# DLRM tower on one core: first two one-hot tables as a couple, and another order of the interaction stage

## The reference

```python
e = jnp.stack([tbl_0[ids[:, 0]], ..., tbl_25[ids[:, 25]]], axis=1)
T = jnp.concatenate([dense[:, None, :], e], axis=1)        # 512 x 27 x 128
Z = jnp.einsum('bnd,bmd->bnm', T, T)                       # all pairs
z = Z[:, iu0, iu1]                                         # 351 pairs, upper triangle
h = jnp.concatenate([z, r_dense], axis=1)
h = jnp.maximum(h @ W_top1 + b_top1, 0.0)                  # 479 -> 512
h = jnp.maximum(h @ W_top2 + b_top2, 0.0)                  # 512 -> 256
y = h @ W_top3                                             # 256 -> 1
```

## Time and profile before

| | us |
|---|---|
| median of 3 runs (118.52, 598.5, 118.72) | 118.72 |
| the profiled execution's own time | 118.53 |
| its span | 116.7 |
| PE busy in the span | 108.4 (93%) |
| DVE busy | 85.6 (73%) |
| ACT busy | 80.9 (69%) |
| POOL busy | 65.3 (56%) |
| DMA, mean over the span | 152 GB/s |
| a gather of POOL, median from issue to landing | 4.1 |
| a move of `Zlow` into `Zt` from POOL, median from issue to landing | 1.9 to 2.0 |

### The profile page before, as it was taken

How to read it: one execution, slowest core, us unless ns; L and a number is a source line. 1 busy time by engine, 2 the same in 40 slices (tenths; PEclk the granted TensorE clock), 3 DMA queues, 4 the chain that set the end, 5 groups by cost and what they waited for, 6 DMA issues and landing times.

```text
span 116.7 us, 2626 instructions
## 1 busy us (share of the span) xinstructions
PE 108.4 (93%) x1008; PEld 91.0 (78%) x1008; DVE 85.6 (73%) x179; ACT 80.9 (69%) x151; POOL 65.3 (56%) x66
## 2 busy tenths in 40 slices
PE   4889799899999999999999999989699998998993
PEld 4757478588688887887888788978599987898990
DVE  5699999889597789969778751499996841567131
ACT  4469990994999999999997794499993602455011
POOL 7387787788777877877787775003063720004000
PEclk9999999999999999999999999999999999999999
DMA  3799749999999529992111112001011110001000
GB/s 74 262 361 406 275 105 411 382 398 363 400 316 380 218 71 367 405 338 65 45 45 32 35 45 60 13 0 26 6 23 51 34 32 6 0 3 21 6 3 1
DMA packets 7751, 17.75 MB, mean 152 GB/s; under 512 B 2078, under 2 KB 3002, under 8 KB 7610
## 3 DMA queue, kind: packets, MB, share of 16 engines
q1 hardware_dynamic: 5770, 14.13, 33.1%
q0 software_dynamic: 1824, 3.25, 9.7%
q10 hardware_dynamic: 144, 0.20, 0.6%
HBM read 17.33 MB, written 0.00 MB: 148 GB/s over the span
## 4 chain that ended last, share of the span: by engine, by line
PE 66%; ACT 11%; DMA 8%; DVE 8%; issue 4%; SPq 1%; ACTq 0%; DVEq 0%
PE work L473 20%; PE work L475 19%; DMA table<-small 8%; PE work L431 8%; PE work L421 6%; PE work L532 5%; ACT Zt L574 4%; PE tp L457 4%; DVE hot L739 3%; PE work L415 3%; ACT t_hi L594 2%; ACT table L566 2%; DVE Zt L574 2%; ACT hot L623 2%; DVE t_lo L708 2%
## 5 line engine op out<-in xcount | busy, mean ns | idle before, releaser
L403 POOL DMA_INDIRECT rows<-tbl,idx x48 | 58.4, 1217 | 18.3 <-issue 13.3
L473 PE MATMUL work<-hot,t_hi 128*128 128x512 f32 x128 | 51.8, 405 | 2.2 <-DVE hot L739 1.1
L475 PE MATMUL work<-hot,t_lo 128*128 128x512 f32 x128 | 50.2, 392 | 0.0
L739 DVE TENSOR_SCALAR hot<-ids_bc,rownum 128x1024 fp32r<-128x1024 int32 (+1 forms) x59 | 38.9, 699 | 7.2 <-PE work L475 7.1
L473 PEld LDWEIGHTS work<-hot,t_hi 128*128 128x128 f32 x128 | 24.0, 188 | 10.8 <-DVE hot L739 2.9
L475 PEld LDWEIGHTS work<-hot,t_lo 128*128 128x128 f32 x128 | 24.1, 188 | 4.4
L594 ACT CAST t_hi<-table 128x1280 fp32r<-128x1280 f32 (+3 forms) x16 | 16.8, 1050 | 5.8 <-DMA table<-small 5.5
L708 DVE TENSOR_TENSOR t_lo<-table,t_hi 128x1280 fp32r<-128x1280 f32 (+3 forms) x16 | 19.5, 1217 | 1.2 <-ACT t_hi L594 1.0
L431 PE MATMUL work<-XT 128*58 128x52 f32 x512 | 15.1, 217 | 2.4 <-ACT Zt L574 1.1
L431 PEld LDWEIGHTS work<-XT 128*58 128x58 f32 x512 | 14.3, 133 | 3.7 <-issue 2.4
L328 POOL DMA_DIRECT2D Zt<-table x9 | 4.7, 531 | 22.1 <-DVE table L566 22.1
(11 more groups left out here) (47 smaller groups left out, 58.1 us busy)
## 6 DMA issues: line engine op xcount, KB each, us to landing
table<-small SPq DMA_DIRECT2D x8, 640.0 KB, 7.9
ids_bc<-ids_oh SPq DMA_DIRECT2D x6, 512.0 KB, 6.1
table<-small SPq DMA_DIRECT2D x4, 512.0 KB, 7.6
w_sb<-w SPq DMA_DIRECT2D x1, 1024.0 KB, 7.7
rows<-tbl,idx POOLq DMA_INDIRECT x48, 4.1
table<-small SPq DMA_DIRECT2D x2, 320.0 KB, 5.0
ids_bc<-ids_oh SPq DMA_DIRECT2D x2, 256.0 KB, 4.5
w_sb<-w SPq DMA_DIRECT2D x1, 512.0 KB, 8.8
```

Source lines behind the costliest of these rows:

```text
L403: nc.gpsimd.indirect_dma_start(rows[:, t, place - FIRST, :], None, tbls[f], bass.IndirectOffsetOnAxis(ap=idx[:, t, place - FIRST:place - F ...
L473: nc.tensor.matmul(bank, t_hi[:, i % PARTS, c * D:(c + 1) * D], hot[:, k % HOTS, :], start=row_chunk(i, c) == 0, stop=False)
L475: last = nc.tensor.matmul(bank, t_lo[:, i % PARTS, c * D:(c + 1) * D], hot[:, k % HOTS, :], start=False, stop=row_chunk(i, c) == n - 1)
L739: nc.vector.tensor_scalar(hot[:, k % HOTS:k % HOTS + n, :], ids_bc[:, ids_slot(f):ids_slot(f) + n, :], rownum[:, v, at:at + 1], None, ALU. ...
```

## The change

`SINGLES` is gone: fields 0 and 1 become a couple like the others. Only the very first pair of chunks (chunks 0 and 1, `LONE` = 2) still gets two one-hots of 512 columns, so that the first matmul needs only field 0's ids. SP loads the ids of fields 0 and 1 first, one after the other. Table 0 is loaded in two parts of 4 chunks each, table 1 in one. ACT makes the last couple of tables 0 and 1 (`ACT_TABLES`), where it made chunks 4, 9 and 14 before. The ids' buffer is used as `f % IDS`: the ids of fields 4 and 5 have free places and their load waits for nothing, where it waited for chunks 0 to 15. The steps `rows` (3, 0) and (3, 1), `dense` 0 and `dense` 2 stand elsewhere in the timeline, DVE copies rows (3, 0) in place of (3, 1), and DVE makes tile 2's ReLU in the midst of its copies of the last gram.

```diff
-VECTOR_ROWS = [(3, 1)]
+VECTOR_ROWS = [(3, 0)]
-HEADED = 2
-HEAD = 3
+HEADED = 1
+HEAD = 4
-SINGLES = 2
+LONE = 2
-ACT_EVERY = 5
-ACT_TABLES = [3, 5, 6, 7, 8, 9, 10, 11, 12, 13]
+ACT_TABLES = [0, 1, 3, 5, 6, 7, 8, 9, 10, 11, 12, 13]
...
-LOW_PARTS.update({(0, 0): (0, 0, HEAD), (0, 4): (0, HEAD, OH_CHUNKS[0]), (0, 5): (1, 0, HEAD),
-                  (1, 1): (1, HEAD, OH_CHUNKS[1])})
+LOW_PARTS = {(i, 4 if OH_CHUNKS[i] == 8 else 6): (i + 1, 0, OH_CHUNKS[i + 1]) for i in range(K_OH - 1)}
+LOW_PARTS.update({(0, 0): (0, 0, HEAD), (0, HEAD): (0, HEAD, OH_CHUNKS[0]), (0, 6): (1, 0, OH_CHUNKS[1])})
...
-    steps += [("dense", 0, 0), ("burst", 0, 0), ("gram", 0, 0), ("burst", 0, 1), ("gram", 0, 1), ("rows", 3, 0),
...
+    steps += [("rows", 3, 0), ("burst", 0, 0), ("gram", 0, 0), ("burst", 0, 1), ("gram", 0, 1), ("dense", 0, 0),
...
@@ sync
-                n = 1 if i < SINGLES else 2
-                if i >= SINGLES + 2:
-                    sp.wait_ge(hot_used, groups_used(first_hot(ids_free(i))))
+                if i >= IDS:
+                    sp.wait_ge(hot_used, groups_used(first_hot(i - IDS + 2)))
...
-            table_ids(0)
+            for f in range(LONE):
+                sp.dma_start(ids_bc[:, f, :], ids_oh[f, :, :]).then_inc(ids_in[f], 16)
@@ scalar
             high_part(0, HEAD, OH_CHUNKS[0])
-            one_hot(mine_in(0)[0])
-            high_part(1, 0, HEAD)
-            distance(1)
-            high_part(1, HEAD, OH_CHUNKS[1])
+            high_part(1, 0, OH_CHUNKS[1])
...
+                    for m in mine_in(i):
+                        one_hot(m)
+                        if i == 0:
+                            distance(1)
+                    if i <= 1:
+                        high_part(i + 2, 0, OH_CHUNKS[i + 2])
@@ vector
+            def units_done(t):
+
+                if t >= 2:
+                    dve.wait_ge(l2_full, t - 1)
+                dve.wait_ge(l1_part, 2 * (t + 1))
+                nc.vector.tensor_scalar(h1[:, t % 2, :, :], l1[:], 0.0, None, ALU.max).then_inc(h1_ready, 1)
...
                     copy_high(nc.vector.tensor_copy, t, i, halves % HALVES, first)
+                    if t == TILES - 1 and i == 1:
+                        units_done(t - 1)
                     if t < TILES - 1 or i == 1:
                         copy_high(nc.vector.tensor_copy, t, i, halves % HALVES, second).then_inc(gram_dve, 1)
```

More of the change, by code:

```diff
@@ L111, in timeline @@
         steps += [("rows", t, g) for t, g in ROWS_AFTER.get(i, [])]
-    steps += [("dense", 0, 0), ("burst", 0, 0), ("gram", 0, 0), ("burst", 0, 1), ("gram", 0, 1), ("rows", 3, 0),
-              ("burst", 1, 0), ("gram", 1, 0), ("rows", 3, 1), ("burst", 1, 1), ("gram", 1, 1), ("burst", 2, 0),
-              ("gram", 2, 0), ("layer1", 0, 0), ("layer1", 0, 1), ("burst", 2, 1), ("gram", 2, 1), ("dense", 1, 0),
[2 rows of a table removed]
+    steps += [("rows", 3, 0), ("burst", 0, 0), ("gram", 0, 0), ("burst", 0, 1), ("gram", 0, 1), ("dense", 0, 0),
+              ("burst", 1, 0), ("gram", 1, 0), ("burst", 1, 1), ("gram", 1, 1), ("burst", 2, 0), ("gram", 2, 0),
+              ("layer1", 0, 0), ("layer1", 0, 1), ("rows", 3, 1), ("burst", 2, 1), ("gram", 2, 1), ("dense", 1, 0),
[2 rows of a table added]
               ("dense", 3, 0), ("layer2", 2, 0), ("layer1", 3, 0), ("layer2", 3, 0), ("turn", 0, 0), ("layer3", 3, 0)]
@@ L607, in distance @@
                 act.wait_ge(ids_in[f], 16)
+                if f == 0:
+                    act.wait_ge(ids_in[1], 16)
                 act.wait_ge(rownum_ready, 2)
@@ L729, in _ @@
                     dve.wait_ge(ids_in[f], 16)
-                    n = 1 if i < SINGLES else 2
-                    for c in range(0, OH_CHUNKS[i], n):
+                    for c in range(OH_CHUNKS[i]):
                         if (i, c) in LOW_PARTS and i + c:
@@ L833 @@
     for i, n in enumerate(OH_CHUNKS):
-        if i < SINGLES:
-            table = chunks[i]
-        else:
-            f = pair_of(i)
-            part = slice((i - f) * n // 2, (i - f + 1) * n // 2)
-            table = np.stack([chunks[f][:, part], chunks[f + 1][:, part]], axis=2)
+        f = pair_of(i)
+        part = slice((i - f) * n // 2, (i - f + 1) * n // 2)
+        table = np.stack([chunks[f][:, part], chunks[f + 1][:, part]], axis=2)
         arrays[f"small_{i}"] = table.reshape(OH_ROWS, n * D)
```

63 lines of the change are left out of this document (24 added, 39 removed), and 4 rows, old and new, of the table steps.

## The result

| | before | after |
|---|---|---|
| median of 20 runs each, us | 119.12 (118.3 to 598.5) | 118.22 (117.35 to 119.57) |
| ratio, with 95% interval | | 0.9932 [0.9909, 0.9956] |
| profiled execution's own time, us | 118.53 | 118.04 |
| its span, us | 116.7 | 116.2 |
| granted TensorE clock | 1.00 | 1.00 |

Here the change brings 0.7%; its repetition further down (again) shows no gain. A ratio compares the executions of each kernel that lie within 1.5% of its fastest, while a median is that of all. The forecast was 117.5 from 118.53, a ratio of 0.991; the median of 118.22 is 0.7 us above it and inside the range of 116.4 to 118.8. Of the 1.1 us forecast behind the lookups, 0.7 came in this profile; and the agreement of the sum hides several terms that missed.

A forecast was written before the change was run, and what follows sets the result against it. TensorE's own work bounds the lookups from 23.7 us, operands the front before, copies the stretch from 75 to 88. Sum: 118.53 + 0 (front) - 1.06 (behind the lookups) = 117.5 us; 8-in-10 range 116.4 to 118.8.

The forecast's parts named there:

- Part 1: Front of the lookups: table 1 lands at 8.5, chunk 12 starts at 14.47; net plus 0.07 us, taken as 0.
- both ends of my range: Table 1's landing: at 7.7 the front gains 0.8 us; landing as late as table 2 did, it loses up to 2.4.
- The gain at chunk 30 and the loss at chunk 12 are the same size: Front: the ended wait for table 5 offsets chunk 12's later start, so the front comes out at 0.
- the front gains: Rival: less DVE work and table 1 landing before 8.5; at 7.9 it gives 0.6 us, 116.9; chance 0.18.
- the front costs half a us: Rival: DVE too close behind TensorE, or half the gain behind the lookups lost: 118.1 us; chance 0.18.
- Part 2: Behind the lookups: rows (3, 0) replace `dense` 0 there; first Gram matmuls at 73.06, 0.25 us earlier.
- plus 0.12 for the handover: Behind the lookups: first Gram matmuls start 0.12 us after ACT's copy is done at 72.94.
- Part 3: Gram copies' pace: burst at 82.82 instead of 83.49, 0.67 us gained; 0.22 to 0.26 left behind rows (3, 1).
- Part 4: `dense` 2 before the burst fills a 0.80 us wait; layer 2 of tile 1 comes 0.66 us earlier.
- Part 5: Tile 2's ReLU ahead of the last four high copies: layer 2 comes 1.07 us earlier, 0.4 of it new.
- Slower, by a late table 1: Rival: each us of later landing from 8.5 delays chunk 12 and the end; at 10.1, 119.1 us; chance 0.06.
- the rival of the clock: Rival: front pauses drop TensorE from 2.4 to 1.2 GHz, chunks 4 to 11 cost 3.7 us more, 121.2; chance 0.02.

The follow-up runs named there:

- again: The changed kernel, unaltered, measured once more: median 119.28 against 119.33 us for the kernel before, ratio 1.0007.
- hots_first: Changed kernel with ACT's first one-hot and distance ahead of table 1's rounding, DVE's `t_lo` of tables 1 and 2 later: 118.71 us, ratio 0.9878 to the kernel before.
- lo_later: Changed kernel with table 2's `t_lo` on DVE moved from chunk 12 to chunk 14: 118.20 us, ratio 0.9912 to the kernel before.
- before_again: The kernel before, unaltered, profiled a second time in one execution: 118.67 us.
- stage_only: Kernel before with only the new order behind the lookups (rows, dense, ReLU): 118.48 against 119.33 us, ratio 0.9917.
- front_only: Changed kernel with the old order behind the lookups, so only the front is new: 120.08 us, ratio 1.0065 to the kernel before.
- waits_turned: Changed kernel with TensorE's five waits before the first Gram matmul reordered, last lookup's copies waited for last: 119.08 us, ratio 0.9983 to the kernel before.
- tbl1_late: Changed kernel with the load of fields 2 and 3's ids ahead of table 1's on SP: 120.51 against 119.39 us, ratio 1.0143 to the kernel before.
- ids45_wait: Changed kernel with fields 4 and 5's ids waiting again, so table 5 loads late: 119.06 against 119.39 us, ratio 1.0000 to the kernel before.
- relu_back: Changed kernel with tile 2's ReLU back behind all DVE copies of the last gram: one execution, 118.39 us.
- dense2_back: Changed kernel with `dense` 2 back behind tile 3's first gram: one execution, 119.08 us.
- rows_back: Changed kernel with tile 3's rows and `dense` 0 back in their old places, DVE copying rows (3, 1): one execution, 118.34 us.

## Why the prediction was right, and where its steps were not

T is table 1's landing, L the end of the last lookup, Y the start of tile 3's layer 1, each in us from one profile; hold is the late release told of below. In hots_first ACT's rounding of table 1 starts at 8.78 without a wait, so T is not seen. In this kernel and in lo_later another order leads to chunk 12, so the distance of 5.96 is not theirs.

| kernel | T | chunk 12 (before: 13) | L | L - T | Y - L | hold |
|---|---|---|---|---|---|---|
| before | | 13.72 | 72.33 | | 37.04 | no |
| before_again | | 14.20 | 72.32 | | 37.19 | no |
| stage_only | | 13.85 | 72.48 | | 36.49 | no |
| front_only | 8.97 | 14.93 | 73.88 | 64.91 | 37.42 | yes |
| after | 7.93 | 13.89 | 72.50 | 64.57 | 36.33 | yes |
| again | 8.65 | 14.62 | 73.17 | 64.52 | 36.42 | yes |
| waits_turned | 7.79 | 13.76 | 72.79 | 65.00 | 36.33 | yes |
| tbl1_late | 10.07 | 16.03 | 73.97 | 63.90 | 36.40 | no |
| ids45_wait | 8.56 | 14.53 | 73.20 | 64.64 | 36.39 | no |
| relu_back | 8.63 | 14.60 | 72.46 | 63.83 | 36.72 | no |
| dense2_back | 9.53 | 15.50 | 73.20 | 63.67 | 36.67 | no |
| rows_back | 8.54 | 14.51 | 72.37 | 63.83 | 36.78 | no |
| lo_later | 8.87 | 13.91 | 73.22 | 64.35 | 36.36 | yes |
| hots_first | | 13.19 | 72.29 | | 36.38 | yes |

**Part 1, the front at 0: right in its sum, by its own steps where nothing else stops TensorE.** The chain from table 1's landing to chunk 12 was worked out as 5.97; it is 5.96 or 5.97 in all nine profiles that have it. The landing was set to 8.5, and the nine profiles that show it with SP's order unaltered up to there have 7.79, 7.93, 8.54, 8.56, 8.63, 8.65, 8.87, 8.97 and 9.53, a middle of 8.6. In the old front, the wait for field 1's ids, from which 8.5 was taken, ended at 8.58, 8.65 and 8.94 in three profiles. With T = 8.54 and no hold (rows_back) chunk 12 starts at 14.51 and the last lookup ends at 72.37; the forecast was 14.47 and 72.3 to 72.4. The equal sum of bytes was thus a good measure of the middle, but not of the spread of 1.7 us, which both ends of my range (7.7, and up to 10.9) had. "The gain at chunk 30 and the loss at chunk 12 are the same size" held: ids45_wait shows 0.8 for the one, and its last lookup, without that gain, ends 0.87 behind that of before (73.20 and 72.33). The profile of the result alone would have misled here: its early T of 7.93 looks as though "the front gains" were true, and again has 8.65. That its last lookup ended at 72.50, so near to the forecast, is luck: T came 0.57 early, and the hold, which the sum did not have, gave back some 0.7.

**What part 1 did not have: the hold.** It brings L - T from 63.8 to 64.5 or more, 0.7 to 1.2 us, in after, again, front_only and waits_turned. In the profiles without it the lookups end at 72.37 and 72.46 with T near 8.6, as before (72.32 to 72.48 with the old front), and at 73.20 with T at 9.53. The half us given back at 41.05 is the hold. In front_only's profile it comes together with a late T. I had a rival "the front costs half a us", but by DVE's being too near to TensorE; this is not the mechanism that showed. DVE's and ACT's one-hots keep up wherever they are released on time.

**Part 2, the first Gram matmul 0.25 earlier: wrong.** The step that failed is "plus 0.12 for the handover". ACT's copy ended 0.59 behind the lookups' end (72.69 + 0.40 - 72.50), as worked out (0.61), but TensorE followed 0.36 behind it. With the waits turned round it is 0.24. Behind L the Gram matmuls start 0.95 later, against 0.98 before, so part 2 gave 0.03. The 0.12 was not read from a handover of this kind: 0.35 to 0.38 us is what it takes in the nine profiles that have the transposes there and the order of waits unaltered.

**Part 3, 0.22 to 0.26 left: too high against the kernel before's profile.** The pace was right: bursts at 78.09 without a wait, 80.62 and 83.15 (9.70 behind the first Gram matmul; 9.76 forecast). But its remainder was in the main part 2's 0.25 handed on, and without that tile 1's layer 1 is 20.38 behind the last lookup against 20.45: 0.07. Up to the start of the burst ahead of it the gain is 0.1 in all profiles (15.82 against 15.91 in the mean). At layer 1 itself four profiles with the old order have 20.45, 20.61, 20.84 and 20.82, ten with the new one 20.37 to 20.53, in the mean 0.25 less. So the size forecast comes out in the mean, but not by the way forecast: most of it is the burst's own length, which is not explained.

**Part 4, 0.40 of its own for `dense` 2: nearly.** dense2_back, one profile, has 36.67, and the mean of the seven profiles with the whole new stage (36.33, 36.42, 36.33, 36.36, 36.40, 36.39, and 36.38 of hots_first) is 36.37: 0.30. What is late next was named right: `dense` 2 waits 0.35 for tile 1's ReLU.

**Part 5, 0.40 for tile 2's ReLU: right.** relu_back, one profile too, has 36.72: 0.35. The four high copies that now stand behind it, the rival's argument, cost nothing.

Parts 4 and 5 and the 0.1 up to the burst make 0.75, and Y - L went from 37.04 to 36.37. Forecast 1.06; against this profile what is missing is mostly parts 2 and 3. With all three profiles of the old stage (37.04, 37.19 and 37.42, 37.22 in the mean) the stage gains 0.84, the longer bursts included.

**The rivals.** "The front gains" needed T before 8.5: it occurs in two profiles of nine, and the hold falls in both. "Slower, by a late table 1" didn't come of itself, but its chain is as told, and tbl1_late's profile shows its price at the last lookup: 73.97 against 72.33, 1.64 us for a T of 10.07, where 1.6 was forecast. The clock stayed at 1.00 in every profile, through single pauses of up to 1.72 us in the front (before chunk 4 in dense2_back). It did not in every execution: besides the five of tbl1_late, the mean granted clock was 0.985 or 0.986 in one of twenty of the changed kernel (119.57 us), three of twelve of front_only and one of twelve of lo_later. It was 0.999 or 1.00 in all 69 executions of the kernel before whose clock is listed and in all 12 of stage_only. So the rival of the clock, given a chance of 0.02, did occur with the new front, most often where table 1 was made to land late. The five executions of tbl1_late lie 0.1 to 1.75 us above the one with a full clock, less than the 3.7 us forecast for it; two of front_only's three took 123.0 and 123.76 us, and no trace tells why.

## What to carry to other kernels

Follow the first pause of the fullest engine back to its load and count the fixed work between: here that distance was 5.96 or 5.97 us in nine profiles, while the landing itself moved by 1.7 us with the order of issue unaltered, so that one profile says little about a load and the distance much. Ask of each wait that a new order fills whether what is moved there was on the path at its old place too: here 0.51 us were gained at tile 0's layer 1, and a tenth of a us was left at the start of the burst behind rows (3, 1). And if a kernel has slack between its pauses, it takes up a late landing (before: chunk 13 half a us later, the same end); a kernel tuned to have none passes it on. Last, look at the clock of every execution and not only of the profiled one: tbl1_late's profile shows 1.00, and five of its six executions had less.
